# Order of row additions, transposes and a PSUM copy in the last GRU layer of a graph network kernel

## The reference

```
def _L0_gnn_ref(z, edge_weight, weight, w_ih, w_hh, b_ih, b_hh, edge_index):
    x = z
    for l in range(3):
        m = x @ weight[l]
        msg = m[src] * edge_weight[:, None]
        agg = segment_sum(msg, dst, num_segments=6250)
        x = _gru_cell(agg, x, w_ih, w_hh, b_ih, b_hh)
    return x
def _L1_gnn_ref(x, edge_index, W0, b0, W1, b1, W2, b2):
    for W, b in ((W0, b0), (W1, b1), (W2, b2)):
        x = relu((x + segment_sum(x[src], dst, num_segments=6250)) @ W.T + b)
    return x
x = _layernorm(x + _L0_gnn_ref(x, ...), axis=-1)
x = _layernorm(x + _L1_gnn_ref(x, ...), axis=-1)
```

## Time and profile before

| | us |
|---|---|
| median of three runs | 3008.77 |
| lowest, highest | 3005.1, 3009.97 |
| the profiled execution | 3003.88 |
| its span, first to last instruction | 3002.1 |
| PE busy in the span | 2915.1 (97%) |
| DVE, ACT, POOL busy | 1514.6, 909.0, 980.7 |

### The profile page before, as it was taken

How to read it: one execution, slowest core, us unless ns; L and a number is a source line. 1 busy time by engine, 2 the same in 40 slices (tenths; PEclk the granted TensorE clock), 3 DMA queues, 4 the chain that set the end, 5 groups by cost and what they waited for, 6 DMA issues and landing times.

```text
span 3002.1 us, 75972 instructions
## 1 busy us (share of the span) xinstructions
PE 2915.1 (97%) x29592; PEld 1909.5 (64%) x29592; DVE 1514.6 (50%) x4498; ACT 909.0 (30%) x2123; POOL 980.7 (33%) x1219
## 2 busy tenths in 40 slices
PE   5999999999999999999999979999999999999998
PEld 4888888888888875555555544454555555555554
DVE  5788888888888824554552255555520010001111
ACT  5666666666666620000002001111220010001111
POOL 3222222222222325777770477777400000000000
PEclk9999999999999999999999989999999999999999
DMA  5555655555555679888895877888568868886884
GB/s 172 230 234 246 248 246 241 232 232 233 246 246 227 251 294 387 319 324 337 321 351 198 340 264 293 320 304 315 205 237 305 305 253 305 305 306 250 309 309 160
DMA packets 150159, 817.85 MB, mean 272 GB/s; under 512 B 19204, under 2 KB 28744, under 8 KB 135208
## 3 DMA queue, kind: packets, MB, share of 16 engines
q1 hardware_dynamic: 121256, 755.56, 64.5%
q0 software_dynamic: 27216, 54.53, 5.7%
q10 hardware_dynamic: 1584, 6.43, 0.5%
HBM read 567.58 MB, written 248.86 MB: 272 GB/s over the span
## 4 chain that ended last, share of the span: by engine, by line
PE 83%; DMA 8%; DVE 4%; issue 2%; POOL 2%; ACT 1%; ACTq 0%; SPq 0%; DVEq 0%; POOLq 0%
PE ps L1081 26%; PE ps L1160 20%; PE ps L883 18%; PE ps L1153 12%; DMA ring<-y_rows,ring 6%; DVE ring L1661 2%; POOL ring L798 2%; PE ps L893 1%; PE ps L894 1%; PE ps L1173 1%; DMA ring<-adj_w 1%; PE ps L1174 1%; PE ps L1060 1%; PE ps L1219 0%; PE ps L896 0%
## 5 line engine op out<-in xcount | busy, mean ns | idle before, releaser
L883 PE MATMUL ps<-ring,Y 128*128 128x448 f32 x2352 | 892.6, 541 | 0.8 <-DMA ring<-adj_w 0.8
L798 POOL DMA_INDIRECT ring<-y_rows,ring x700 | 676.6, 967 | 388.0 <-DVE ring L1661 164.5
L1081 PE MATMUL ps<-ring,Y 128*128 128x448 f16 x4116 | 780.6, 352 | 0.0
L1537 ACT ACTIVATE ring<-ps 128x392 f16<-128x392 f32 (+1 forms) x1568 | 654.8, 507 | 289.6 <-PE ps L1153 280.7
L883 PEld LDWEIGHTS ps<-ring,Y 128*128 128x128 f32 x2352 | 448.0, 191 | 437.5 <-issue 435.1
L1081 PEld LDWEIGHTS ps<-ring,Y 128*128 128x128 f16 x4116 | 402.7, 98 | 373.8
L1160 PE MATMUL ps<-ring,Y 128*128 (+1 forms) x2744 | 614.7, 366 | 0.4 <-ACT shared L1499 0.4
L1661 DVE SCALAR_TENSOR_TENSOR ring<-ring 128x128 f32<-128x128 f32 x1384 | 400.2, 348 | 356.8 <-DMA ring<-y_rows,ring 353.3
L1160 PEld LDWEIGHTS ps<-ring,Y 128*128 128x128 f32 x2744 | 491.3, 190 | 15.4 <-ACT shared L1499 0.8
L1153 PEld LDWEIGHTS ps<-shared 64*128 64x128 bf16 x18816 | 335.3, 94 | 118.4 <-ACT ring L1537 86.3
L1936 DVE TENSOR_TENSOR shared<-shared 128x400 bf16<-128x400 bf16 x1176 | 396.2, 392 | 0.0
(11 more groups left out here) (177 smaller groups left out, 1394.1 us busy)
## 6 DMA issues: line engine op xcount, KB each, us to landing
ring<-adj_w SPq DMA_DIRECT2D x72, 2688.0 KB
adj_w<-ring SPq DMA_DIRECT2D x56, 2744.0 KB, 12.3
ring<-adj_h SPq DMA_DIRECT2D x42, 2800.0 KB, 9.4
ring<-adj_h SPq DMA_DIRECT2D x42, 2688.0 KB, 9.2
adj_h<-ring SPq DMA_DIRECT2D x56, 1372.0 KB, 5.0
ring<-adj_w SPq DMA_DIRECT2D x24, 2912.0 KB
ring<-y_rows,ring POOLq DMA_INDIRECT x700
y_rows<-Y ACTq DMA_DIRECT2D x2, 3136.0 KB, 15.2
```

The source lines that it names most:

```text
L798: pool.indirect_dma_start(out=run_rows[:, i % ROW_BUFS, :], out_offset=None, in_=y_rows, in_offset=bass.IndirectOffsetOnAxis(ap=run_edges[ ...
L883: mm = pe.matmul(ps[:, bank, 0:GW], Y[:, h, :], ring[:, s, :, h - h0, :], start=(h == 0), stop=(last and h == TILES - 1))
L1081: mm = pe.matmul(ps[:, par, 0:GW], part[:, h, :], ring_h[:, par, s, :, h - h0, :], start=(h == 0 and part is Y_high), stop=(h == TILES - 1 ...
L1537: act.activation(strip[:, :, c0:c0 + UNIT * WIN].rearrange("p h (d j) -> p d h j", d=WIN), psum_unit(a)[:, :, kind, :, :].rearrange("p d j ...
```

## The change

Three edits, all in layer three. DVE: slot -1 of the row additions stands behind the reduction L1701 and ahead of the wait for the bound, where it stood behind the centred weights. TensorE: the transposes of pair i-1 stand behind all four slabs of group 2i+1, for the last i behind three slabs; they stood behind two. ScalarE: inside the loop the copy of group 2i+1 stands ahead of the deviations and the normalisation; it stood behind them. Line numbers behind the first edit grow by one, behind the DVE edit by three.

```diff
@@ def last_gru_layer (TensorE)
                 for i in range(DENSE // 2):
-                    aggregate(n0 + 2 * i + 1, 1, slabs=range(2), skipped=SKIPPED)
+                    early = range(SLABS - 1 if i == DENSE // 2 - 1 else SLABS)
+                    aggregate(n0 + 2 * i + 1, 1, slabs=early, skipped=SKIPPED)
                     if i:
                         flip_sums(i - 1, (6, 7))
-                    aggregate(n0 + 2 * i + 1, 1, slabs=range(2, SLABS), skipped=SKIPPED)
+                    aggregate(n0 + 2 * i + 1, 1, slabs=range(early.stop, SLABS), skipped=SKIPPED)
@@ def last_gru_layer (ScalarE)
                 with act.Fori(1, DENSE // 2 - 1) as i:
                     n = n0 + 2 * i
+                    evac(n + 1, 1, SKIPPED)
                     deviate(i - 1)
                     keep_norm(i - 1, (6, 7))
-                    evac(n + 1, 1, SKIPPED)
                     update(n)
@@ def find_scale (DVE)
                 sc_step(l, k, dve.tensor_reduce(x_top[:, :], x_tops[:, :], mybir.AxisListType.X, ALU.max))
+                if l == 0:
+                    add_rows(1, -1)
                 dve.wait_ge(s_bnd, l + 1 + (l > 0))
@@ def last_gru_layer (DVE)
                 find_scale(0, 6, 2)
                 scale_centred_weights()
-                add_rows(1, -1)
                 sum_group(n0, 0)
                 take_centred_weights(7)
```

## The result

The changed kernel took 3012.98 us (median of 20 runs, 3010.01 to 3017.29) against 3005.8 us for the kernel before on the same chip (20 runs, 3004.08 to 3010.28). The ratio is 1.002, with a 95% interval of 1.0013 to 1.0027: slower by 0.2%, a small loss but one clear of the spread, where I had forecast no change. The time lies inside my range (3001 to 3014), but the range had been laid around a before of about 3007: against the same chip's 3005.8 the difference is +7 us, and I had given a loss one chance in ten.

What follows compares the result with a forecast made beforehand. The prediction took layer three's chain of row gathers, additions and statistics to bound the kernel. Its terms, 0 + 0 - 2.4 + 2.4 = 0 us, gave 3007.5 us, between the earlier executions' mean and median, range 3001 to 3014.

Steps and rivals of the forecast that it cites:

- What bounds the kernel: Layer three: the chain of row gathers, DVE additions and ScalarE's normalisation sets the pace; TensorE's five waits, 25.7 us, are shadows.
- Part one, the early slot: DVE, layer three: 30 rounds added ahead of the bound only move the stall; next slot still starts at 1734.3: 0 us.
- Part two, the transposes: TensorE, layer three: transposes behind all four slabs remove a 16.15 us wait but idle time returns elsewhere: 0 us.
- Part three, the copy: ScalarE, layer three: copying the odd group's sums ahead of the deviations takes 0.59 us off the path four times: -2.4 us.
- The landing term: Odd slots' ends, layer three: last gathers land slower inside slab refills, 0.6 us each at four ends: +2.4 us.
- The walk through the slab ends: Layer three's new slab order: last gathers fall 4.6 to 7 us into an 8 us refill, nearer its end.
- Rival C: Layer three: every odd slot's last gather lands inside the slab stream, up to +12.4 us, 3020 us; 0.08 at 6 us or more.
- Rival D, the clock: TensorE after the wait at 2150.72: a longer wait leaves its clock slow, up to +1 us; no chance of its own.
- The sign that I had named: First count matmul, at 2178.4 before, forecast within 2 us of its place; a move over 4 us means wrong.

Runs made afterwards that it cites:

- before with halves: Kernel before with only the first half of each slab transferred in layer three, TensorE still multiplying all tiles: 3004.83 us, ratio 0.9996.

## Why the prediction was wrong

**What bounds the kernel**: right. The chain through gathers, additions and statistics holds layer three, and TensorE's waits are its shadow: the edit removed 25.7 us of them and others came, 13.0 ahead of the odd groups' gates, 8.0 ahead of the last transposes, and 11.9 in place of 4.0 ahead of L947.

**Part one, the early slot**: right, 0 us (1.0003). The bound's step ran at 1695.25 (forecast: by 1697.1 at the latest), L1722 waited 31.5 us (forecast: about 30), the slot began at 1733.98 (forecast: 1734.3 within 0.5).

**Part two, the transposes**: "On the path: 0 us" was right for the waits and wrong for their consequence, which I had put in a term of its own, below. TensorE's idle time from 1734 to 2150 was 26.6 us (forecast 25 to 32), its four waits for the mix in the stage 2.4 to 4.2 us each (forecast 1 to 3), and its longest wait 11.87 us, ahead of L947 at 2156 (forecast near 2110; the one there was 7.95, from 2118).

**Part three, the copy**: right mechanism, about 0.41 us each in place of 0.59, so -1.7 us in place of -2.4. The ratios of the two kernels that have the copy and not the TensorE edit, 0.9993 and 0.9991, stand for -2.1 and -2.7, with intervals that reach to no change.

**The landing term**: the step that failed, by size. I had "0.6 us each, +2.4 us" with bounds of 0 and 3.7 each. The walk through the slab ends that stood behind it was about right: it put the last gathers 4.6 to 7 us behind the end of a slab, and they were issued 4.7 to 8.2 us behind a slab's request. The price that I gave to that place was wrong. I took it as near the end of a refill and so nearly free. Measured, the odd slots end later by 2.1, 1.0, 2.9 and 0.8 us, 6.8 us at the four ends in place of 2.4, and by 0.7 at the fifth end, slot 9's, which I had not counted. The time from the issue of the last gather to the statistics says the same: 5.3, 4.6, 6.1 and 4.1 us at the four ends in place of 3.2, 3.4, 3.1 and 3.3. Even at 8 us behind the request there is no pause to land in, because the next request comes at 9.0 us. Rival C was the truth at about a half of its price, and its chance of 0.08 too small. It needed 2.1 us each at four ends against the copy's gain to reach 6 us; the ends came to 7.5 us at five, less 1.7 for the copy: 5.8 us. That the time still fell inside my range is luck: before was 1.7 us faster than the value I had started from.

**Rival D, the clock**: the granted clock behind the last wait was 0.50 in 2156.2 to 2162.7, and 1.4 us of the profile's difference lie there. But L947 took 1.19 us in two kernels without the TensorE edit as well (early slot alone, copy alone), so I leave it out of the cause.

The sign that I had named, "if the first count matmul moves by more than 4 us", showed: it moved by 7.

## What to carry to other kernels

When a chain of small gathers sets the pace beside a bulk stream, ask of each edit on the engine that paces the stream where in the refill the gather that is waited for will land: an edit that only moves that engine's waits costs nothing there and still moves the stream. If that engine is re-set by a wait once per period, the phase is nearly the same in every period (read here from two traces), so the cost comes at every period with the same sign, here 0.7 to 2.9 us at each of five. A gather that is issued late in a refill is not free where the next refill follows at once. Give the loss a real chance, rather than pricing the landing near its lower bound. And moving idle time is no gain until the instruction that holds the chain (here a 0.29 us copy that waits 31 us ahead of ready work) is itself moved: with that line moved as well, the changed kernel was 26 us faster than before on the one chip where it was timed.

## What the runs showed of the hardware

A gather of 64 KB landed in 2.6 to 2.7 us where the DMA engines were 0.21 to 0.26 busy and in 5.5 to 6.0 us where they were 0.93 to 0.98 busy, in the same stage of two orders of one kernel. TensorE's four transposes L947 took 0.68 us after 3.4 to 4.0 us of waiting in three profiles (before, before with halves, the changed kernel without the TensorE edit) and 1.19 us in others after 2.6 to 13.3 us: the clock granted there differs between executions of almost equal order. And a program can be 11% slower on some chips (3335 to 3350 us against 3004 to 3006), at a mean granted clock of 0.94 in place of 0.99 and with long waits for issue at its matmuls (166.5 us at L883 in one profile, none there in before and the changed kernel); a difference of 0.2% cannot be carried from one such chip to another.
